# Attention's results stored undivided, with channels in rows, and divided in the gating stage

## The reference, cut to what matters

```python
q = (src @ Wq + bq).reshape(B, T, NHEAD, HEAD_DIM)      # 16 heads of 16 channels
scores = jnp.einsum('bqhd,bkhd->bhqk', q, k) * scale
probs = jax.nn.softmax(scores, axis=-1)
out = jnp.einsum('bhqk,bkhd->bqhd', probs, v).reshape(B, T, d)
attn_out = out @ Wo + bo
x = _ln(src + attn_out, ln1_g, ln1_b)
ff = _moe(x, gW, gb, W1, b1, W2, b2)                    # top 2 of 8 experts per row
```

## Time and profile before

| | us |
|---|---|
| median of 3 runs | 3698.08 (3696.91 to 3700.52) |
| the profiled execution's own time | 3687.84 |
| its span in the trace | 3686.1 |
| PE, DVE, ACT, POOL busy | 3230.1, 2950.5, 2059.5, 1196.9 |
| head attention, first pass to last store | about 221 to 1620 |
| gating stage | about 1621 to 1742 |

### The profile page before, as it was taken

One profiled execution on the slowest core, in us unless ns is written; L12 is line 12 of the kernel. 1 busy time (PEld: TensorE's weight loads), 2 busy tenths in 40 slices (PEclk: granted clock), 3 DMA queues, 4 the chain that ended last, 5 costly groups with the idle time before them and its releaser, 6 DMA issues. The chain is left out here.

```text
span 3686.1 us, 87940 instructions
## 1 busy us (share of the span) xinstructions
PE 3230.1 (88%) x34874; PEld 1852.7 (50%) x34875; DVE 2950.5 (80%) x4783; ACT 2059.5 (56%) x2972; POOL 1196.9 (32%) x974
## 2 busy tenths in 40 slices
PE   4889999999999999984999765997799999967876
PEld 1543333333333333344666542343677787746665
DVE  5778999999999999925566354776699999948986
ACT  0316777777777777762011155665565757434553
POOL 0310000000000000006011370000899999927775
PEclk8868999999999999996999877998899999989998
DMA  1552112020202020035222353333544434231110
GB/s 57 194 151 24 21 29 45 5 45 5 46 10 58 20 56 6 5 115 203 82 65 65 112 168 124 119 119 128 150 127 122 136 106 134 78 120 52 57 34 18
DMA packets 223121, 296.00 MB, mean 80 GB/s; under 512 B 72872, under 2 KB 159536, under 8 KB 220592
## 3 DMA queue, kind: packets, MB, share of 16 engines
q1 hardware_dynamic: 209872, 261.98, 25.0%
q0 software_dynamic: 6144, 17.05, 1.4%
q10 hardware_dynamic: 6752, 11.96, 0.9%
HBM read 174.35 MB, written 115.95 MB: 79 GB/s over the span
## 5 line engine op out<-in xcount | busy, mean ns | idle before, releaser
L999 DVE TENSOR_REDUCE att_maxima<-att_ps_m 128x1 f32<-128x512 f32 x2048 | 1285.6, 684 | 66.6 <-PE att_ps_m L1055 65.1
L954 ACT ACTIVATE att_probs<-att_ps_s 128x1024 f32<-128x1024 f32 x1024 | 999.7, 1022 | 282.7 <-PE att_ps_o L1084 269.8
L1084 PE MATMUL att_ps_o<-att_probs,held_vs 128*32 128x256 f32 x8192 | 658.8, 393 | 4.9 <-ACT att_probs L954 0.6
L2426 POOL TENSOR_TENSOR ss_ch<-ss_h,ss_c_rep 128x1024 f32<-128x1024 f32 x256 | 602.2, 2439 | 9.4 <-DVE ss_h L2513 9.4
L1055 PE MATMUL att_ps_m<-held_ks,held_qs 48*128 48x512 f32 x2048 | 585.1, 512 | 14.0 <-PEq L60 13.4
L2545 PE MATMUL ss_ps_u<-ss_diag,ss_dx_t 128*32 128x128 f32 x16384 | 473.4, 274 | 29.5 <-DMA ss_dx_t<-scratch_dx_t 16.0
L2545 PEld LDWEIGHTS ss_ps_u<-ss_diag,ss_dx_t 128*32 128x32 f32 x16384 | 452.6, 111 | 85.7 <-issue 69.0
L1055 PEld LDWEIGHTS att_ps_m<-held_ks,held_qs 48*128 48x128 f32 x2048 | 238.3, 188 | 458.1 <-DVE att_maxima L999 392.4
L1070 PE MATMUL att_ps_s<-held_qs,held_ks 50*128 50x512 f32 x2048 | 454.7, 405 | 2.8 <-ACT att_probs L954 0.8
L2465 ACT ACTIVATE ss_decay<-ss_delta,ss_a_neg 128x1024 f32<-128x1024 f32 x256 | 293.8, 1148 | 228.6 <-DVE ss_h L2513 205.9
L1084 PEld LDWEIGHTS att_ps_o<-att_probs,held_vs 128*32 128x32 f32 x8192 | 162.7, 108 | 362.5 <-issue 341.3
(11 more groups left out here) (394 smaller groups left out, 4469.1 us busy)
## 6 DMA issues: line engine op xcount, KB each, us to landing
ss_delta<-scratch_delta SPq DMA_DIRECT2D x256, 128.0 KB, 3.1
held_qs<-scratch_q SPq DMA_DIRECT2D x96, 128.0 KB, 4.6
held_ks<-scratch_k SPq DMA_DIRECT2D x96, 128.0 KB, 4.9
ex_x<-scratch_sorted_x SPq DMA_DIRECT2D x72, 132.0 KB, 2.0
scratch_sorted_y<-ex_y SPq DMA_DIRECT2D x72, 128.0 KB, 1.7
scratch_q<-held_parts SPq DMA_DIRECT2D x16, 512.0 KB, 4.6
scratch_k<-held_parts SPq DMA_DIRECT2D x16, 512.0 KB, 5.5
moe_w_w<-in_W SPq DMA_DIRECT2D x16, 512.0 KB
```

Of the source, the lines that this page charges most:

```text
L954: act.activation(probs[:, (2 * n + pair) % 4, :, :], ps_s[pair][:, :, :], ACT.Exp, scale=HD ** -0.5).then_inc(exp_done, 1)
L999: dve.tensor_reduce(maxima[:, j, at:at + 1], ps_m[plan.bank(key)][:, :], AX.X, ALU.max).then_inc(maxed, 1)
L1084: mm = pe.matmul(ps_o[h * VW:(h + 1) * VW, cols], vs[st // QC % 2][:, kt, h * VW:(h + 1) * VW], probs[:, (2 * n + h // 2) % 4, h % 2, cols ...
L2426: pool.tensor_tensor(ch[:, w.n % (CH_GROUPS * DQ), :], h[:, w.n % H_SLOTS, :], c_rep[:, w.ng, :], ALU.mult).then_inc(s["ch_ready"], 1)
```

## The change

- The scratch tensor `heads` (rows by channels) is replaced by `outs` (256 channels by 4096 rows, undivided) and `inv` (16 heads by 4096 rows, the inverted sums).
- Head attention: `turn_out`, `copy_turned` and `divide` are gone, and the transposes' place in the rotation of the banks. `o_sb` has two slots. SP stores the 16 channel rows of each of 4 heads from `o_sb` (four DMAs), then spreads the row of sums of each head, 512 numbers, over 32 partitions of 16 numbers (four DMAs). VectorE inverts [128, 16] after key tile 6 (`INVERT`). SP stores the inverses (four DMAs), after `store_shift`.
- Gating: SP loads a group of `outs` directly as `heads_t` (two slots), and the inverses in eight DMAs, each of which repeats one row over the 16 channels of a head (one buffer). VectorE multiplies the two (`divide`) ahead of `add_src`. `turn_heads` and `copy_heads` are gone.
- The columns of the values behind the channels are all ones, set by one memset for each buffer instead of two.

```diff
-        self.heads = dram("heads", (T, C))
+        self.outs = dram("outs", (C, T))
+        self.inv = dram("inv", (HEADS, T))
...
-                    pool.memset(by_head[:, :, HD:HD + 1], 1.0).then_inc(v_set, 1)
-                    pool.memset(by_head[:, :, HD + 1:VW], 0.0).then_inc(v_set, 1)
+                    pool.memset(by_head[:, :, HD:VW], 1.0).then_inc(v_set, 1)
...
-                if st > 0 and kt == 1:
-                    order.append(("out", st - 1))
...
+INVERT = 6
...
+                def store_outs(st):
+                    head, cols = places_of(st)
+                    sp.wait_ge(o_copied, st + 1)
+                    for h in range(QH):
+                        sp.dma_start(scratch.outs[(head + h) * HD:(head + h + 1) * HD, cols], o_sb[h * VW:h * VW + HD, st % 2, :]).then_inc(outs_stored[st % 2], 16)
+                    if st > 0:
+                        sp.wait_ge(sums_inverted, st)
+                    for h in range(QH):
+                        sp.dma_start(sums[h * VW:(h + 1) * VW, :], o_sb[h * VW + HD:h * VW + HD + 1, st % 2, :]).then_inc(sums_spread, 16)
+
+                def store_inv(st):
+                    head, cols = places_of(st)
+                    sp.wait_ge(sums_inverted, st + 1)
+                    for h in range(QH):
+                        sp.dma_start(scratch.inv[head + h:head + h + 1, cols].rearrange("o (p j) -> (o p) j", p=VW),
+                                     inv[h * VW:(h + 1) * VW, :]).then_inc(inv_stored, 16)
...
                         sp.wait_ge(pv_done, st * KT)
                         load_quad(st // QC + 1)
-                    store_heads(st - 1)
+                    store_outs(st - 1)
                     if st + 1 < STEPS:
                         store_shift(st + 1)
+                    store_inv(st - 1)
...
-                        if st > 0 and kt == 4:
-                            divide(st - 1)
...
-                    act.activation(o_sb[:, :], ps_o[:, :], ACT.Copy).then_inc(o_copied, 1)
+                    if st >= 2:
+                        act.wait_ge(outs_stored[st % 2], st // 2 * QH * 16)
+                        act.wait_ge(sums_spread, (st - 1) * QH * 16)
+                    act.activation(o_sb[:, st % 2, :], ps_o[:, :], ACT.Copy).then_inc(o_copied, 1)
...
-                        if st > 0 and kt == 2:
-                            copy_turned(st - 1)
...
-                    dve.wait_ge(o_t_ready, st + 1)
+                    dve.wait_ge(sums_spread, (st + 1) * QH * 16)
                     if st > 0:
-                        dve.wait_ge(heads_ready, st)
-                    dve.reciprocal(sums[:, :], o_t[:, :, HD]).then_inc(sums_ready, 1)
+                        dve.wait_ge(inv_stored, st * QH * 16)
+                    dve.reciprocal(inv[:, :], sums[:, :]).then_inc(sums_inverted, 1)
...
-                        if st > 0 and kt == 3:
+                        if st > 0 and kt == INVERT:
                             invert_sums(st - 1)
...
-                        if st > 0 and kt == 1:
-                            turn_out(st - 1)
...
+                def load_inv(g):
+
+                    if g > 0:
+                        sp.wait_ge(heads_t_ready, g)
+                    by_row = scratch.inv[:, g * GN:(g + 1) * GN].rearrange("(k e) n -> e k n", k=KC)
+                    for e in range(HEADS // KC):
+                        sp.dma_start(inv[e * HD:(e + 1) * HD, :, :], over(by_row[e:e + 1, :, :], [HD, KC, GN])).then_inc(inv_loaded, 16)
...
                 load_heads(0, 0)
+                load_inv(0)
...
                     if g + 1 < GROUPS:
+                        load_inv(g + 1)
                         load_src(g + 1, (g + 1) % 2)
...
+                def divide(g, slot):
+
+                    dve.wait_ge(heads_loaded[slot], (g // 2 + 1) * 16)
+                    dve.wait_ge(inv_loaded, (g + 1) * HEADS // KC * 16)
+                    dve.tensor_tensor(heads_t[:, slot, :, :], heads_t[:, slot, :, :], inv[:, :, :], ALU.mult).then_inc(heads_t_ready, 1)
...
-                run_stages(dve, GROUPS, (add_src, 1), (find_places, 4), (shift_logits, 3), (find_scale, 1), (take_best, 3), unroll=True)
+                run_stages(dve, GROUPS, (divide, 0), (add_src, 1), (find_places, 4), (shift_logits, 3), (find_scale, 1), (take_best, 3), unroll=True)
...
-                run_stages(act, GROUPS, (copy_heads, 0), (scale_xa, 2), (norm, 1), (exp_logits, 3), (scale_y, 1), unroll=True)
+                run_stages(act, GROUPS, (scale_xa, 2), (norm, 1), (exp_logits, 3), (scale_y, 1), unroll=True)
...
-                run_stages(pe, GROUPS, (turn_heads, 0), (count, 4), (turn_rows, 2), (product, 0), (logits, 2), unroll=True)
+                run_stages(pe, GROUPS, (count, 4), (turn_rows, 2), (product, 0), (logits, 2), unroll=True)
```

More of the change, by code:

```diff
@@ L825, in head_attention @@
         probs = r.sb("probs", [P, 4, 2, GN])
-        o_sb, o_t = r.sb("o_sb", [P, GN]), r.sb("o_t", [P, GT * QH, VW])
-        sums = r.sb("sums", [P, GT * QH])
-        heads = r.sb("heads", [P, GT, QH * HD])
+        o_sb = r.sb("o_sb", [P, 2, GN])
+        sums, inv = (r.sb(n, [P, GN // VW]) for n in ("sums", "inv"))
         ps_s = [r.ps(f"ps_s{i}", [P, 2, GN]) for i in range(2)]
@@ L897, in _ @@
                         store_x1(st - 2 - A_LOADS)
-                store_heads(STEPS - 1)
-                sp.wait_ge(heads_stored, STEPS * 16)
+                store_outs(STEPS - 1)
+                store_inv(STEPS - 1)
+                for slot in range(2):
+                    sp.wait_ge(outs_stored[slot], STEPS // 2 * QH * 16)
+                sp.wait_ge(inv_stored, STEPS * QH * 16)
                 sp.wait_ge(b1_laid, 16)
@@ L913, in split_shift @@
                     pool.tensor_tensor(m_parts[:, 1, :], m_t[:, :], m_parts[:, 0, :].bitcast(F32), ALU.subtract).then_inc(m_split, 1)
[L915 to L919, removed]
-                    pool.tensor_tensor(heads[:, :, :].rearrange("p t (h d) -> p (t h) d", d=HD), o_t[:, :, 0:HD],
-                                       over(sums[:, :].unsqueeze(2), [P, GT * QH, HD]), ALU.mult).then_inc(heads_ready, 1)
                 def lay_values(g):
@@ L1041, in bank_free @@
                         pe.wait_ge(m_copied, 2 * (last[1] + 1))
-                    elif last[0] == "out":
-                        pe.wait_ge(o_t_ready, last[1] + 1)
                     else:
@@ L1087, in values @@
                         mm.then_inc(pv_done, 1)
-                def turn_out(st):
-                    bank_free(("out", st))
-                    pe.wait_ge(o_copied, st + 1)
-                    for t in range(GT):
-                        mm = pe.transpose(ps_m[plan.bank(("out", st))][:, t * P:(t + 1) * P], o_sb[:, t * P:(t + 1) * P], ident[:, :])
-                    mm.then_inc(o_turned, 1)
                 for i in range(UNITS):
@@ L1454, in turn_rows @@
                     mm.then_inc(rows_turned, 1)
-                def turn_heads(g, slot):
-                    pe.wait_ge(heads_loaded[slot], (g // 2 + 1) * 16)
-                    pe.wait_ge(heads_t_ready, g)
-                    for t in range(GT):
-                        for k in range(KC):
-                            mm = pe.transpose(ps_h[:, k, t * P:(t + 1) * P], heads[:, slot, t, k * P:(k + 1) * P], ident[:, :])
-                    mm.then_inc(heads_turned, 1)
                 def product(g, slot):
@@ L1470, in product @@
                         for k in range(KC):
-                            mm = pe.matmul(ps_y[:, t, :], heads_t[:, k, t * P:(t + 1) * P], wo[:, k, :], start=k == 0, stop=k == KC - 1)
+                            mm = pe.matmul(ps_y[:, t, :], heads_t[:, slot, k, t * P:(t + 1) * P], wo[:, k, :], start=k == 0, stop=k == KC - 1)
                     mm.then_inc(y_ready, 1)
```

35 lines of the change are left out of this document (11 added, 24 removed).

## The result

The changed kernel takes 3820.89 us (median of 6 runs, 3808.42 to 3829.85), the kernel before beside it 3698.86 us (3696.91 to 3701.52): a ratio of 1.0313, 95% interval 1.0288 to 1.0338, slower by 122 us. The forecast was 3792.

The account below looks back on a forecast made before the run. The prediction took VectorE to bound the attention and POOL's scatters the gating stage. Its terms, -17 + 60 + 40 + 5 + 6 = +94 us on a median of 3698, gave 3792 us, range 3736 to 3840.

Parts of the forecast that it names:

- The bound: Attention: VectorE bounds it with almost no slack; whatever stops VectorE for a time lengthens the kernel by that time.
- Transposes gone: Attention: VectorE's 0.56 us stop at the transposes goes in 30 steps, 17 us less.
- The waits: Attention, six quad-loading steps: VectorE waits for sums queued behind the loads, 10 us each, 60 us in all.
- The halved clock: Attention, behind the six stalls: idle TensorE's clock halves for 16 us each, 40 us in all, bounds 15 and 68.
- End of the attention: After the last copy of a result: the round trip of sums and inverses ends 4 to 7 us later, 5 taken.
- Gating: Gating stage: first scatter 6 us later, VectorE then even with POOL at 10.2 us a group; bounds 2 and 14.
- The chain of one buffer: Gating stage: a group's inverse loads wait for the previous group's multiply, making some 9 us a group.
- list of signs: Expected profile: six waits of 9 to 11 us, half clock behind them, steps of 41.3 us, first scatter 10 us later.
- Sum: Whole kernel: -17 + 60 + 40 + 5 + 6 = +94 us on the median 3698, so 3792 us.
- A: Rival, attention: stalls come, but the clock holds or returns at once; +54 to +66, about 3758 us; chance 0.20.
- B: Rival, attention: sums land in time and nothing stalls; -6 or -11, 3687 to 3692 us; chance 0.08.
- C: Rival, gating stage: VectorE waits for inverses each group, POOL's chain has holes; 14 us more, 3806 us; chance 0.10.

Follow-up runs that it names:

- experiment 1: Changed kernel with INVERT = 12 instead of 6, so VectorE inverts the sums six key tiles later: 3684.0 us, ratio 0.9991 to the kernel before.
- experiment 5: Changed kernel, INVERT still 6, with SP issuing stores and spreads of the sums ahead of a quad's 25 loads: 3707.81 us, ratio 1.0002 to the kernel before.
- second profile: The unaltered changed kernel run and profiled again on another chip: 3806.58 us, ratio 1.0281 to the kernel before.
- experiment 3: Changed kernel with INVERT = 12 and the old gating stage, reading the source tensor instead of the attention's results: 3674.1 us, ratio 0.9957 to the kernel before.
- experiment 6: Kernel before with only the new gating stage, reading queries in place of results and inverses: 3715.0 us against 3705.6, ratio 1.0031.
- experiment 7: Changed kernel with INVERT = 12 and two buffers for the gating stage's inverses instead of one: 3704.8 us, ratio 0.9994 to the kernel before.
- experiment 12: Changed kernel with INVERT = 12 and the gating multiply cut to 8 of 1024 elements a partition: 3698.66 us, ratio 0.9988 to the kernel before.
- experiment 11: The kernel before, unaltered, profiled once more on a later chip to look for holes in its scatters: 3692.29 us, one run.
- experiment 4: Changed kernel, INVERT still 6, plus ten unread TensorE matmuls in each of the six loading steps: 3763.25 us, ratio 1.0197 to the kernel before.
- experiment 2: Changed kernel with INVERT = 8 instead of 6, so VectorE inverts two key tiles later: 3766.26 us, ratio 1.0203 to the kernel before.

## Why the prediction was right

The direction and the mechanism were right, and the time lies 29 us above the forecast, within its range. Step by step:

- *The bound.* Right. Whatever VectorE lost in the attention lengthened the kernel, and 0.56 us of transposes gone made a step 0.56 us shorter.
- *Transposes gone, -17.* Measured -17.9 and -18.5 us (experiments 1 and 5 against before's first profile).
- *The waits, +60.* Measured 60.8 us in six, 10.1 each. Two details were off and cancelled: the sums came 10.8 us after the values' load instead of 12.4 (the spread was there 1.2 us after its last issue, not 1.9), and VectorE came 1.4 us sooner against that load. The reason for the held issue was read correctly from the earlier trace rows, and experiment 5 shows that the order in the queue is the whole of it. One support was weaker than it looked: the 8.6 us to landing count from the start of the issue and hold the 5.66 us of the held issue, so they show little of an order behind the loads. In the kernel after the sums landed 1.2 us behind their last issue; what the traces show is the hold at issue.
- *The halved clock, +40, bounds 15 and 68.* This is the term that was mis-sized: 65 us in the first profile, 41 in the second. The place, the level and the loss per us (0.42) held; the length did not. The middle was taken between 26.3 and 5.8 us, though the row on the same kind of work said 26.3, and the measured mean is 162.6 / 6 = 27 us. The second profile, 41 / 0.42 / 6 = 16 us a wait, gave the forecast's figure. A size that varies from 8.5 to 52 us within one execution could not be had closer from two rows. The granted clock of the six runs goes with their times, 0.911 in the two quickest and 0.903 in the slowest. But their spread of 21 us is no proof of it: experiment 1, without the stall, spreads over 22 us in ten runs.
- *End of the attention, +5.* Measured 4.5 in the profile and 4.8 in experiment 3.
- *Gating, +6, bounds 2 and 14.* Measured 9.4 by time and 9.8 by the first scatter (experiment 6), 10.7 in the profile after (15.2 less the 4.5). The chain of one buffer, given as the reason, is not it (experiment 7). The multiply's share is 2 to 4 us (experiment 12). With the 4.5 of the attention's end the first scatter came 15.2 us later, where the prediction's list of signs says 10.
- *Sum.* With the measured terms -17.9 + 60.8 + 65 + 4.8 + 9.4 = 122 us, and the medians differ by 122. That the two agree to the microsecond is luck: the profiled execution, from which the waits and the clock are taken, lies 3826.66 - 3698.86 = 128 us above before's median. The second profile's terms give -17.9 + 61.8 + 41 + 4.8 + 9.4 = 99; its execution lies 3801.02 - 3705.59 = 95 us above before's median, the median of its runs 101. So the terms explain the time to some 6 us, if the longer scatters (discussed under experiment 11) are in the kernel before as well, which isn't shown.

Of the rivals, A (the clock holds) is the case that experiment 4 built by hand: 1.0197 instead of 1.0281 to 1.0313; left to itself the clock fell in all six waits. B (no stall) is what experiments 1 and 5 are: against its forecast of -6 to -11 stand their -3 and +1 us, as the gating stage costs more than thought. C foresaw holes in POOL's chain, and there are some, about 14 us of them in the profile after. But the largest one stands behind a VectorE that waits, but not for inverses (last section), the 4.09 us hole comes 30 us after the last multiply by them, and on two of the chips the holes are nearly absent. The ratios show no effect of them.

## What to carry to other kernels

A small transfer that an in-order engine will wait for belongs ahead of a block of loads in its queue, or the waiting instruction belongs as far behind as its consumer allows: here one constant or three moved lines were worth 3% of the kernel. When a wait idles TensorE in a dense stage, add a second price for the clock, take its size from the recovery that this kind of work shows in the trace, and give it a wide range; half the wait did not bring half of that price here (53 us against 41 and 65). Work removed from a bound engine is only won if what replaces it does not come back on another stage's critical path, as 13 us won here came back as 10 in the gating stage.

## What the hardware showed that was not expected

The clock's recovery on the same instruction mix, at the same place of the loop, took from 8.5 to 52 us in one execution, and in experiment 2 all six gaps, of 4.02 to 7.30 us, were followed by a low clock, as were all six of 8.97 to 10.3 us in the kernel after. In experiment 4 gaps of 2.74 and 2.23 us were followed by a low clock too, and one of 1.34 us behind 8.85 us of matmuls was, for 10.2 us; the other three waits had none.

In the largest hole of the gating stage TensorE's matmuls of 8 columns were issued one at a time, without a recorded wait. Timeline of TensorE, with VectorE's next sum as the last row, then the window of all engines:

```profile
1811.75 0.17 PE L1482 MATMUL ao_ps_c<-ao_both,ao_all_ones 128*128 128x8 bf16 x1 [1.05 <-issue]
1812.47 0.19 PE L1484 MATMUL ao_ps_c<-ao_both,ao_earlier 128*128 128x8 bf16 x1 [0.55 <-issue]
1813.88 0.17 PE L1482 MATMUL ao_ps_c<-ao_both,ao_all_ones 128*128 128x8 bf16 x1 [1.23 <-issue]
...
1816.83 1.23 DVE L1322 TENSOR_TENSOR ao_y<-ao_ps_y,ao_src 128x1024 f32<-128x1024 f32 x1 [4.55 <-remote]
```

```profile
1808.00:1818.00 10.00, 2.35 (x20) 2.02 (x21) 3.67 (x7) 0.00 (x0) 4.99 (x6) 0.58 1.05 394
```

VectorE's sum waits, by the code, for the load of the source, for the product and for ScalarE's rows, and for none of these small matmuls; "remote" says that the profile doesn't name what released it. The DMA engines were full then, at 394 GB/s. They are as full in experiment 1's gating stage (383 GB/s from 1675 to 1695), where no such hole stands, so the load alone does not explain it; the cause stays open.
